# The value matmuls of two tiles inside a step's score matmuls instead of behind them

## What is computed

```python
xn = _layernorm(x)
qkv = xn @ attn_qkvw + attn_qkvb            # q, k, v: 32 heads x 2048 x 32
scores = einsum('bhqd,bhkd->bhqk', q, k) * scale
probs = softmax(scores, axis=-1)
ctx = einsum('bhqk,bhkd->bhqd', probs, v)
x = x + (ctx @ attn_ow + attn_ob) + ffn(xn)
```

## Time and profile before

| | us |
|---|---|
| median of 3 runs | 2508.06 |
| lowest and highest of the runs | 2505.8, 2508.11 |
| time of the profiled execution | 2506.15 |
| span of its instructions | 2504.3 |
| TensorE, matmuls busy | 2473.9 (99%) |
| TensorE, weight loads busy | 1599.2 (64%) |
| VectorE busy | 1500.8 (60%) |
| ScalarE busy | 1225.2 (49%) |
| GpSimd busy | 1636.6 (65%) |

### The profile page before, as it was taken

The page is one execution under the profiler, slowest core; times in us unless marked ns, Lnnn a source line. Parts: engine busy times, 40 slices in busy tenths (PEclk is TensorE's granted clock), DMA queues, the critical chain, the costliest instruction groups (busy, mean ns, idle before and its releaser), DMA issues. The chain is left out here.

```text
span 2504.3 us, 34205 instructions
## 1 busy us (share of the span) xinstructions
PE 2473.9 (99%) x12856; PEld 1599.2 (64%) x12856; DVE 1500.8 (60%) x2525; ACT 1225.2 (49%) x2311; POOL 1636.6 (65%) x560
## 2 busy tenths in 40 slices
PE   7999999999999999999999999999999999999999
PEld 5788888888855555555555555555555555548887
DVE  7511110104588888888888888888888888632221
ACT  6211111110066676667667667666666766771000
POOL 0111011321189999999999999999999999962111
PEclk8999999999999999999999999999999999999999
DMA  5233335324367777777777877777777787664332
GB/s 168 93 126 126 126 120 161 101 80 126 97 171 164 150 159 166 161 149 167 165 152 158 168 151 160 165 161 148 166 166 152 158 168 151 131 151 148 117 108 85
DMA packets 175903, 359.50 MB, mean 144 GB/s; under 512 B 90880, under 2 KB 116432, under 8 KB 144720
## 3 DMA queue, kind: packets, MB, share of 16 engines
q0 software_dynamic: 22752, 165.69, 33.6%
q1 hardware_dynamic: 153008, 191.94, 26.9%
HBM read 127.42 MB, written 63.70 MB: 76 GB/s over the span
## 5 line engine op out<-in xcount | busy, mean ns | idle before, releaser
L1206 DVE TENSOR_REDUCE part_max<-ps_bc 128x1 f32<-128x512 f32 x1984 | 1213.8, 681 | 255.5 <-PE ps_bc L1071 255.5
L1184 ACT ACTIVATE probs<-ps_bc 128x512 f32<-128x512 f32 x1920 | 971.3, 625 | 344.7 <-PE ps_bc L1059 341.0
L1021 POOL TENSOR_TENSOR psum<-psum,probs 128x2048 f32<-128x2048 f32 x128 | 599.9, 4687 | 25.2 <-ACT probs L1184 20.4
L1021 POOL TENSOR_TENSOR psum_p<-psum_p,probs 128x2048 f32<-128x2048 f32 x125 | 587.3, 4698 | 21.4 <-ACT probs L1184 16.5
L1059 PE MATMUL ps_bc<-q,k 128*128 128x512 f32 x1344 | 545.2, 410 | 1.5 <-ACT probs L1184 1.5
L1071 PE MATMUL ps_bc<-k,q 128*128 128x512 f32 x1344 | 535.8, 400 | 0.8
L1059 PEld LDWEIGHTS ps_bc<-q,k 128*128 128x128 f32 x1344 | 251.1, 187 | 237.6 <-issue 135.7
L1089 PE MATMUL ps_bc<-probs,v 128*32 128x512 f32 x2640 | 319.4, 598 | 0.0
L357 POOL TENSOR_TENSOR wlo<-wraw,whi 128x1024 fp32r<-128x1024 f32 x20 | 48.0, 2398 | 397.1 <-ACT whi L532 397.1
L1059 PE MATMUL ps_bc<-qk 128*128 128x512 f32 x704 | 286.7, 410 | 2.0 <-PEq L89 1.7
L1071 PEld LDWEIGHTS ps_bc<-k,q 128*128 128x128 f32 x1344 | 253.0, 188 | 47.1 <-DVE part_max L1206 21.6
(11 more groups left out here) (150 smaller groups left out, 2753.8 us busy)
## 6 DMA issues: line engine op xcount, KB each, us to landing
psum<-probs POOLq DMA_DIRECT2D x80, 1024.0 KB, 7.8
psum_q<-probs POOLq DMA_DIRECT2D x78, 1024.0 KB, 7.6
qk<-qk_scr SPq DMA_DIRECT2D x66, 256.0 KB, 7.3
qk_scr<-ehi SPq DMA_DIRECT2D x16, 1024.0 KB, 3.9
qk_scr<-elo SPq DMA_DIRECT2D x16, 1024.0 KB, 6.7
k<-qk_scr SPq DMA_DIRECT2D x63, 256.0 KB, 4.1
q<-qk_scr SPq DMA_DIRECT2D x63, 256.0 KB, 7.9
wraw<-wcat SPq DMA_DIRECT2D x21, 512.5 KB, 7.4
```

The lines of the kernel that those rows point to most:

```text
L1021: pool.tensor_tensor(acc[:, :], first[:, :], tile(h, t)[:, :], ALU.add).then_inc(pool_done, 1)
L1184: act.activation(tile(h, t)[:, b * NQ:(b + 1) * NQ], ps[:, st_bank(n), :], ACT.Exp, scale=SCALE).then_inc(exp_done, 1)
L1206: dve.tensor_reduce(part_max[hn % 2][:, tn, b:b + 1], ps[:, ring_bank(u), :], AX_X, ALU.max) \
```

## The change

The value matmuls of a step become a function. In heads 1 to 30 and steps 2, 4, 8, 10, 12 and 14 it is called when two of the step's four pairs are issued, otherwise, as before, behind all four. In steps 0 and 6 and in heads 0 and 31 nothing changes. In odd steps the function issues nothing.

```diff
             def step(h, t):
                 ahead = maxima_at(h, t)
+                def pair_of_values():
+                    if t == 0 and h >= 1:
+                        values(h - 1, TT - 2)
+                        values(h - 1, TT - 1)
+                    if t % 2 == 0 and t >= 2:
+                        values(h, t - 2)
+                        values(h, t - 1)
+                        if h == LAST:
+                            last_sums(t - 2)
+                            last_sums(t - 1)
+
+                middle = QB // 2 if 1 <= h < LAST and t >= 2 and t != SUMS_AT else QB
                 for b in range(QB):
+                    if b == middle:
+                        pair_of_values()
                     scores_t(h, t, b)
                     for u in ahead[b:b + 1]:
                         scores(*u)
                 for u in ahead[QB:]:
                     scores(*u)
-                if t == 0 and h >= 1:
-                    values(h - 1, TT - 2)
-                    values(h - 1, TT - 1)
-                if t % 2 == 0 and t >= 2:
-                    values(h, t - 2)
-                    values(h, t - 1)
-                    if h == LAST:
-                        last_sums(t - 2)
-                        last_sums(t - 1)
+                if middle == QB:
+                    pair_of_values()
                 if t == SUMS_AT and h >= 1:
                     sums(h - 1)
```

## The result

The changed kernel takes 2514.99 us in the median of 8 runs (2512.86 to 2517.47), the one before 2507.32 (2505.8 to 2508.29): ratio 1.003, 95% interval 1.0021 to 1.0038. The forecast was 2517.2, in a range of 2508.5 to 2523; it put +9.1 us on a median of 2508.06 from three runs, and the measured difference is +7.7. The profiled execution took 2515.30 us with a span of 2513.5, which stand against 2506.15 and 2504.3. TensorE's mean granted clock was 0.998 in it and 0.996 before (1 is the 2.4 GHz level), so the clock is not the cause.

The account below looks back on a forecast made before the run. TensorE's own stream was taken as the bound. Ten-pair stalls 5.9 plus flip 3.8 less relief 0.6 gave +9.1 us on a median of 2508.06, so 2517.2, in a range of 2508.5 to 2523.

Parts of the forecast that it names:

- The bound: Whole kernel: TensorE's own instruction stream sets the pace, 48.0 us a head, with about 0.1 us a head unexplained.
- the rule of the ring: Four-bank maxima ring: a maxima matmul can't stream until the reduction four places back ends, plus T = 0.16 us.
- The ten-pair runs: Ten score pairs between value blocks, steps 4 to 6 and 14 to next 0: 59 stalls of 0.10, 5.9 us.
- M9: Tenth maxima score matmul of a ten-pair run: ready at 4.50 us, bank free at 4.60, so 0.10 late.
- The flip: Next head's matmul in the maxima ring, now two pairs later in its run: stall 0.31 not 0.18, 3.8 us.
- The relief: Small unexplained waits on TensorE, at most 0.1 us a head: 0.02 x 30 = 0.6 us taken as gain.
- at the edge, as now: Runs of six and eight pairs: the last score matmul is ready just as its bank frees, at 3.34; no stall.
- cost nothing: GpSimd's tiles 2 and 4 start up to 1.9 us later, tile 7 0.84, taken back each head at tile 2.
- over 10 us: Step 6's sums read GpSimd's last add over 10 us after it ends, so its lag stays hidden.
- Rival 3: GpSimd becomes the bound as chained DMAs wait for one another: up to 45 us slower, 2562; chance 0.05.
- The first: Rival: ten-pair runs don't stall and only the flip costs, +1.7 up to +5 us, 2509.8 to 2513; chance 0.20.
- the second: Rival: the flip's new place lets VectorE catch up and small waits go, at most 7.3 us faster, 2500.8; chance 0.07.

Follow-up runs that it names:

- with one pair: The changed kernel with only the step's fourth score pair issued behind the value block, instead of two pairs; 2512.47 us, ratio 1.0023 to the kernel before.

## Why the prediction was right, point by point

**The bound, and the rule of the ring.** Right. Pair pitch 0.463, entry 0.33 and exit 1.85 are unchanged, and the ring's rule with T = 0.16 gave the length of runs of 6 to 11 pairs to 0.01 to 0.02, with the shortened reductions as proof that VectorE is the cause.

**The ten-pair runs.** 59 x 0.10 = 5.9 us was forecast; 4.935 against 4.83 undisturbed is 0.105, 6.2 us. Of the signs, the load of M9 came 0.05 behind m5 as said, but what follows the load stands 0.43 later and not 0.33: it is a value matmul, whose usual distance of 0.33 gets the 0.10 on top.

**The flip.** 29 x 0.13 = 3.8 forecast; 4.334 against 4.205, 3.7 us, and moving it back gave 3.96.

**The relief** was mis-sized. 0.6 us was taken, and heads 1 to 29 rose by 6.7, not by 9.9, so 3.2 us of small waits went. The step that fails calls eight pairs free "at the edge, as now". Undisturbed they take 0.33 + 7 x 0.463 + 0.33 = 3.90; before, they took 3.915, seven times a head, which is the 0.1 us a head that the prediction could not explain, and in the changed kernel they take 3.897. So the whole of it went and not a fifth. One run of head 20 (4.50 us long before) is 0.6 of the 3.2; which waits made up the rest was not taken apart.

**GpSimd** at "cost nothing" was wrong in two ways. First, a new delay arises at tile 6 in most heads: its chained DMA waits for that of tile 3, for which the arithmetic had no term, so that tile 7 starts 0.3 to 2.4 us later and not 0.84. In the changed kernel a wait still takes this back in every head from 2 to 29, at tile 2 in 16 of them as forecast, or at tile 4, which starts within 0.4 us of its exponentials in all; with all blocks in the middle it is no longer taken back. Second, "over 10 us" does not hold in head 31, whose steps are shorter: before the change the chained DMA of tile 14 landed there 0.26 us ahead of the sums that read it, and it now lands 1.6 us later, which costs 1.5. Rival 3 named the mechanism (chained DMAs wait for each other, GpSimd has 1 us of room), with a price far too high and at tile 9, not 6. In the changed kernel the lag costs 1.5 us; in the variants of the changed order that free TensorE it eats a good part of the gain: head 31 alone takes back 1.8 of 4.5 us with one pair and 4.9 of 5.3 with all blocks in the middle.

**The total** was forecast at +9.1 and measured at +7.7; by parts of the profiled executions it is 9.9 of stalls, less 3.2, plus 1.5, 8.2, and differences of single executions. The errors in the relief and in head 31 partly cancel. The span came out at 2513.5 (forecast 2513.4), which is partly luck: the profiled pair lies 9.2 apart, 0.9 of it outside heads 1 to 29 and 31.

**Rivals.** The first (no stall at M9) and the second (faster) fell: M9 was late 59 times. T = 0.06, a load that waits only for the signal, is out as well, since M9 was late. By 216 ns a matmul, which the Trainium skill gives in TensorE: Matmul & The Clock Gate, "Back-to-back issue gap", M9 would have been 0.38 late as an estimate; the trace has 0.105.

## What to carry to other kernels

Where two engines meet in a ring of few banks, a stretch has a length up to which the slower one is hidden; work out the first late item from the two pitches and the ring's depth, and cut the stretches evenly. A small odd item in the ring costs least as the first of a stretch, behind the work that lets the other engine drain, and most at its end: the flip made its run 0.02 us longer than 3.90 as its first item, 0.30 behind M3, 0.43 behind M4, M5 or M6, and 0.56 at the end, there with the wait for the row maxima. And if an engine in the background is busy 97%, a reordering that saves the bound engine a microsecond has to be read on that engine too, in its in-order waits for DMAs and in the last, shorter stage.

## What was unexpected of the hardware

A transpose of 16 columns of weights in front of a score matmul cost almost nothing when it opened a run (S0 0.03 behind it, the run no longer), 0.12 within one. Two DMAs from different queues that begin together traded time: the megabyte of tile 3 went from 9.2 to 10.5 us, the query load from 7.9 to 5.0; and one of 8 KB, the negated maxima, from 1.8 to 4.6 us in the median when the chained DMA of tile 9 came to lie over it.
